# Expert layers of a macaron block on one core: gate and up in chunks of 256, 512 and 512 tokens in place of four of 320

## The reference, cut to what matters

```python
x = x + 0.5 * _L0_ffn_ref(_layernorm(x), router_w, wg, wu, wd)
x = x + _L0_attn_ref(_layernorm(x), Wq, bq, Wk, bk, Wv, bv, Wo, bo)
x = x + 0.5 * _L0_ffn_ref(_layernorm(x), router_w, wg, wu, wd)
...
def _L0_ffn_ref(x, router_w, wg, wu, wd):   # E = 8 experts, top 2, capacity 1.25 * N / E
    ...
    disp = jnp.zeros((E, capacity + 1, D), x.dtype).at[se, pos].set(xf[st])
    disp = disp[:, :capacity]
    g = jnp.einsum('ecd,edf->ecf', disp, wg)
    u = jnp.einsum('ecd,edf->ecf', disp, wu)
    eo = jnp.einsum('ecf,efd->ecd', jax.nn.silu(g) * u, wd)
    ...
    out = jnp.zeros_like(xf).at[st].add(contrib)
```

## Time and profile before

| | us |
|---|---|
| median of 3 runs | 1755.51 (1755.17 to 1757.69) |
| the profiled execution's span | 1752.8 |
| PE busy | 1586.2 |
| DVE busy | 1129.1 |
| ACT busy | 885.1 |
| POOL busy | 755.7 |

### The profile page before, as it was taken

One profiled execution on the slowest core, in us unless ns is written; L12 is line 12 of the kernel. 1 busy time (PEld: TensorE's weight loads), 2 busy tenths in 40 slices (PEclk: granted clock), 3 DMA queues, 4 the chain that ended last, 5 costly groups with the idle time before them and its releaser, 6 DMA issues.

```text
span 1752.8 us, 40278 instructions
## 1 busy us (share of the span) xinstructions
PE 1586.2 (90%) x14505; PEld 1252.3 (71%) x14505; DVE 1129.1 (64%) x2523; ACT 885.1 (50%) x1624; POOL 755.7 (43%) x611
## 2 busy tenths in 40 slices
PE   5649999999999999976899764999999999999997
PEld 4536878787877878764788653687878787777876
DVE  7898484858576574626788788746374645556461
ACT  5645454544444454527676564445454544544452
POOL 7403525344443426036666650452534444342503
PEclk9999999999999999997999755999999999999999
DMA  8754616263443525038777460452615243443502
GB/s 266 255 156 125 137 42 133 54 137 57 110 75 92 91 76 92 4 44 192 163 158 160 128 224 5 125 106 62 136 51 120 67 111 67 96 76 87 85 7 31
DMA packets 276544, 184.12 MB, mean 105 GB/s; under 512 B 175339, under 2 KB 263157, under 8 KB 276469
## 3 DMA queue, kind: packets, MB, share of 16 engines
q1 hardware_dynamic: 245748, 140.50, 29.6%
q0 software_dynamic: 30720, 42.62, 16.0%
HBM read 91.04 MB, written 55.06 MB: 83 GB/s over the span
## 4 chain that ended last, share of the span: by engine, by line
PE 78%; DVE 10%; ACT 3%; issue 3%; POOL 3%; DMA 3%; SPq 1%; DVEq 0%; POOLq 0%; ACTq 0%
PE bank L1637 48%; PE bank L1649 24%; ACT xt L763 2%; PE bank L1615 1%; PE bank L1583 1%; DVE bank L338 1%; DMA xs<-x_d 1%; DVE xn L1046 1%; PE bank L1690 1%; DVE xn L1135 1%; POOL rows L530 1%; PE bank L1525 1%; POOL w_d L540 1%; POOL unit_buf L535 1%; PE bank L1722 1%
## 5 line engine op out<-in xcount | busy, mean ns | idle before, releaser
L1637 PE MATMUL bank<-xT,rows 128*128 128x320 f16 x3072 | 500.5, 299 | 1.0 <-DVE w_u L1025 1.0
L1637 PE MATMUL bank<-xT,w_u 128*128 128x320 f16 x3072 | 500.8, 299 | 0.0
L1262 DVE SCALAR_TENSOR_TENSOR unit_buf<-bank,sc_cur,unit_buf 128x320 f32<-128x320 f32 x512 | 281.9, 551 | 327.3 <-PE bank L1637 318.6
L812 ACT ACTIVATE unit_buf<-bank,sc_cur 128x320 f32<-128x320 f32 x512 | 269.5, 526 | 375.4 <-PE bank L1637 373.2
L1649 PE MATMUL bank<-w_d,xs 128*128 128x256 f16 x3840 | 421.8, 273 | 0.0
L1649 PEld LDWEIGHTS bank<-w_d,xs 128*128 128x128 f16 x3840 | 375.7, 98 | 44.3
L1637 PEld LDWEIGHTS bank<-xT,w_u 128*128 128x128 f16 x3072 | 300.6, 98 | 116.7
L1637 PEld LDWEIGHTS bank<-xT,rows 128*128 128x128 f16 x3072 | 291.6, 98 | 109.6 <-issue 2.0
L460 POOL DMA_INDIRECT gat<-rows_d,id_next x160 | 183.3, 1146 | 311.1 <-issue 253.9
L1268 DVE TENSOR_TENSOR xs<-unit_buf,xs 128x320 f16<-128x320 f32 x512 | 246.9, 482 | 2.2
L818 ACT ACTIVATE xs<-unit_buf 128x320 f16<-128x320 f32 x512 | 235.6, 460 | 10.4 <-DVE unit_buf L1262 10.4
(11 more groups left out here) (238 smaller groups left out, 1618.7 us busy)
## 6 DMA issues: line engine op xcount, KB each, us to landing
rows_d<-rows SPq DMA_DIRECT2D x32, 512.0 KB, 3.7
raw_gu<-in_L_ffn_wg SPq DMA_DIRECT2D x16, 1024.0 KB, 6.7
raw_gu<-in_L_ffn_wu SPq DMA_DIRECT2D x16, 1024.0 KB
raw_d<-in_L_ffn_wd SPq DMA_DIRECT2D x16, 1024.0 KB, 5.2
x_d<-xs SPq DMA_DIRECT2D x1, 8192.0 KB, 32.8
out_x<-xs SPq DMA_DIRECT2D x16, 512.0 KB, 3.5
xs<-in_L_attn_x SPq DMA_DIRECT2D x7, 1024.0 KB, 7.4
xs<-x_d SPq DMA_DIRECT2D x6, 1024.0 KB, 6.4
```

The lines of the kernel that those rows point to most:

```text
L812: act.activation(act_s[:, u % 2, :], bank[u % 2][:, 0:CW], ACT.Silu, scale=sc_cur[:, 3:4]).then_inc(S.s_ready, 1)
L1262: dve.scalar_tensor_tensor(h32[:, u % HB, :], bank[2 + u % 2][:, 0:CW], sc_cur[:, 4:5], act_s[:, u % 2, :], mult, mult).then_inc(S.h32_rea ...
L1637: mm = pe.matmul(bank[2 * m + u % 2][:, 0:CW], wgu[m][:, w, k, f * P:(f + 1) * P], xT[:, a * KD + k, c * CW:(c + 1) * CW], start=(j == 0 a ...
```

## The change

The three chunks are of two, four and four row blocks: 256, 512 and 512 tokens, so an expert has 24 units. PE issues 96 matmuls of 256 columns and 192 of 512 for gate and up, where it issued 384 of 320. `act_s` moves from `unit_buf` to `xn`, and `h32` takes all of `unit_buf`. The first expert begins on two row blocks turned by PE, and each weight's split is awaited by itself, just before its first matmul. The down weight's split moves to units 8 to 12, and the list pieces, maxima, list read and gathers get new unit numbers.

```diff
-    CH = 4
-    CW = C // CH
+    CHUNKS = ((0, 2), (2, 6), (6, 10))
+    CH = len(CHUNKS)
+    SPAN = [slice(a * P, z * P) for a, z in CHUNKS]
+    CW = max(z - a for a, z in CHUNKS) * P
...
-    BY_PE = 3
-    PARTS = ((0, 1), (2,), (3, 4), (5, 6, 7), (8, 9))
+    BY_PE = 2
+    PARTS = ((0, 1), (2, 3), (4, 5), (6, 7), (8, 9))
+    CHUNK_OF = [c for c, (a, z) in enumerate(CHUNKS) for _ in range(a, z)]
...
-        AMAX_JOIN = 25
-        AMAX_AT = {u: (k // 4, k % 4) for k, u in enumerate((7, 10, 13, *range(16, 25)))}
-        PIECE_AT = {5 + i + i // 2: i for i in range(LP)}
+        AMAX_AT = {11: (0,), 16: (1, 2), 17: (3,), 18: (4, 5), 19: (6, 7), 20: (8, 9), 21: (10, 11)}
+        AMAX_JOIN = 22
+        PIECE_AT = {u: i for i, u in enumerate((2, 4, 6, 8, 10, 13, 14, 15))}
...
-        READ_AT = 20
+        READ_AT = 18
+        DOWN_HI_AT = (8, 11)
+        DOWN_LO_AT = (9, 12)
...
-                            pool.wait_ge(S.u_ready, units + READ_AT + 2 + s)
+                            pool.wait_ge(S.u_ready, units + READ_AT + 1 + s // 2)
...
-                        if units is not None and (s == 0 or READ_TILL[s] > READ_TILL[s - 1]):
-                            sp.wait_ge(S.u_ready, units + FT * (READ_TILL[s] + 1))
+                        if units is not None and s == CHUNKS[c][0]:
+                            sp.wait_ge(S.u_ready, units + FT * (c + 1))
...
-                act.activation(act_s[:, u % 2, :], bank[u % 2][:, 0:CW], ACT.Silu,
+                w = wide(u)
+                act.activation(act_s[:, u % 2, 0:w], bank[u % 2][:, 0:w], ACT.Silu,
...
-                    if u in (0, FT // 2):
-                        pe.wait_ge(S.gu_lo, 4 * e + (2 if u == 0 else 4))
-
                     for m, (free, done) in enumerate(((S.s_ready, S.g_ready), (S.h32_ready, S.u_ready))):
                         pe.wait_ge(free, UNITS * e + u + 1)
+                        if u in (0, FT // 2):
+                            pe.wait_ge(S.gu_lo, 4 * e + 2 * (u > 0) + m + 1)
                         for j, (a, w) in enumerate(HALVES):
                             for k in range(KD):
-                                mm = pe.matmul(bank[2 * m + u % 2][:, 0:CW], wgu[m][:, w, k, f * P:(f + 1) * P],
-                                               xT[:, a * KD + k, c * CW:(c + 1) * CW],
+                                mm = pe.matmul(bank[2 * m + u % 2][:, 0:wide(u)], wgu[m][:, w, k, f * P:(f + 1) * P],
+                                               xT[:, a * KD + k, SPAN[c]],
```

More of the change, by code:

```diff
@@ L324, in col, with wide @@
             return ap[:, i:i + n] if isinstance(i, int) else ap[:, bass.ds(i, n)]
+        def wide(u):
+            a, z = CHUNKS[u // FT]
+            return (z - a) * P
         def wait_for(eng, sm, n):
@@ L626, in turn_rows @@
                     for s in blocks:
-                        c = NEEDED_BY[s]
-                        if units is not None and (s == 0 or READ_TILL[s] > READ_TILL[s - 1]):
-                            sp.wait_ge(S.u_ready, units + FT * (READ_TILL[s] + 1))
+                        c = CHUNK_OF[s]
+                        if units is not None and s == CHUNKS[c][0]:
+                            sp.wait_ge(S.u_ready, units + FT * (c + 1))
                             settle(sp)
-                        if units is not None and s and NEEDED_BY[s - 1] < c:
-                            sp.wait_ge(turned[c - 1], 16 * NEEDED_BY.count(c - 1) * (n + S.first + 1))
-                            settle(sp)
+                            if c:
+                                sp.wait_ge(turned[c - 1], 16 * CHUNK_OF.count(c - 1) * (n + S.first + 1))
+                                settle(sp)
                         sp.dma_start_transpose(xT[:, :, s * P:(s + 1) * P], gat[:, s, 0:2 * D]).then_inc(turned[c], 16)
@@ L1261, in unit @@
                 dve.wait_ge(S.h_ready, UNITS * e + u + 1)
[L1262 to L1263 removed]
+                w = wide(u)
+                dve.scalar_tensor_tensor(h32[:, u % HB, 0:w], bank[2 + u % 2][:, 0:w], sc_cur[:, 4:5],
+                                         act_s[:, u % 2, 0:w], mult, mult).then_inc(S.h32_ready, 1)
             def unit_lo(S, e, u):
@@ L1297, in expert @@
                         continue
-                    if u in AMAX_AT and not S.scaled:
-                        m, i = AMAX_AT[u]
-                        ch.mark(weight_amax(S, m, n, i))
+                    for k in () if S.scaled else AMAX_AT.get(u, ()):
+                        ch.mark(weight_amax(S, k // 4, n, k % 4))
                     if u in PIECE_AT:
@@ L1659, in ffn @@
                 spin(bank[7], wgu[0][:, 0, 0, 0:512], 12)
-                for j in range(2):
-                    pe.wait_ge(gathered[j], 16 * len(PARTS[j]) * (S.first + 1))
-                    for s in PARTS[j]:
-                        for c in range(2 * KD):
-                            i = pe.transpose(bank16[s][:, c * P:(c + 1) * P], gat[:, s, c * P:(c + 1) * P], ident16[:, :])
-                        i.then_inc(S.counted, 1)
-                    spin(bank[7], wgu[0][:, 0, 0, 0:512], 2)
+                pe.wait_ge(gathered[0], 16 * len(PARTS[0]) * (S.first + 1))
+                for s in PARTS[0]:
+                    for c in range(2 * KD):
+                        i = pe.transpose(bank16[s][:, c * P:(c + 1) * P], gat[:, s, c * P:(c + 1) * P], ident16[:, :])
+                    i.then_inc(S.counted, 1)
+                spin(bank[7], wgu[0][:, 0, 0, 0:512], 2)
                 with pe.Fori(0, E - 1) as e:
```

38 lines of the change are left out of this document (18 added, 20 removed).

## The result

The changed kernel takes 1792.0 us (median of 4 runs, 1788.5 to 1793.7), the kernel before 1755.96 beside it: a ratio of 1.0199, 95% interval 1.0187 to 1.021. That is 36 us slower. The forecast was 4 us slower, 1759.6 us, and its range ended at 1766. The sign was right and the size wrong by a factor of nine; nearly all of the loss lies where the prediction said "no gap during down parts". The profiled execution of the changed kernel spans 1786.7 us, against 1752.8 before: 33.9 us to find.

A forecast was written before the change was run, and what follows sets the result against it. TensorE was taken to bound the kernel, at 90% of the span. One pass: 1.4 + 6 x 0.15 - 0.25 = 2.05, two passes 4.1, so 1755.51 becomes 1759.6 us; range 1754 to 1766.

The forecast's parts named there:

- no gap during down parts: Down parts of the experts: PE would show no gap there, nor at chunk starts.
- Step 1: Gate and up of each expert: fewer, wider matmuls take 51.91 us in place of 52.16, a gain of 4.0 in all.
- Step 2: Gate and up units: VectorE and ScalarE keep up with 512-wide units, and 256-wide ones are close but covered; price 0.
- Step 3: First expert: PE starts earlier, at about 136.9, gaining 0.65 us, with some 0.17 given back at up of unit 2.
- step 4: First expert of each pass: PE waits 2.1 us for POOL's hot_v at the first list piece; the expert is 1.4 longer.
- Step 5: Six middle experts per pass: PE waits 0.40 us for hot_v at the first list piece, net +0.15 each.
- rival A: POOL is in time in the middle experts and only the first experts wait: -0.7, 1754.8 us; chance 19%.
- Step 6: Moved transposes, gathers, scatters and weight scales around the down part cost nothing: price 0, margin 1.7 us.
- The scales are ready about 9.8 into it: Pass 1: weight scales come about 9.8 us into the down part; PE needs block 3's eviction only if after about 11.5.
- rival C: Another wait starts: scales later than 11.5 in pass 1, hot_v blocked, or VectorE behind; about 1766 us; chance 14%.
- The scatters catch up: Down part: gathers end about 4 us into it; scatters have 2.62 us each for 1.9 of work.

The follow-up runs named there:

- g4: Changed kernel with list pieces moved to units 6 to 10 and 13 to 15, and the weight maxima's two transfers one row pair earlier in SP's queue: 1749.9 us, ratio 0.9984.
- e4: Changed kernel with list pieces at units 5 to 12 and the list read at unit 15, so gathers come earlier: 1749.3 us, ratio 0.9983.
- g3: Changed kernel with list pieces at units 5 to 12 and the list read at unit 15, run on another chip: 1749.8 us, ratio 0.9981.
- h3: Changed kernel with list pieces at units 5 to 12 and the list read at unit 15, run in the last job: 1749.8 us, ratio 0.9984.
- e2: Changed kernel with list pieces moved to units 6 to 10 and 13 to 15, gathers left where they are: 1776.4 us, ratio 1.0138.
- f1: Changed kernel unaltered, run again on a third chip: 1780.4 us, ratio 1.0146.
- g1: Changed kernel unaltered, run again on a fourth chip: 1780.7 us, ratio 1.0157.
- h1: Changed kernel with only the weight maxima's two transfers moved one row pair earlier in SP's queue: 1757.5 us, ratio 1.0028.
- e1: Changed kernel with list pieces at units 2, 4, 5 to 10 and the list read at unit 13, so gathers come earlier: 1756.0 us, ratio 1.0021.

## Why the prediction was wrong

**Step 1, right.** Gate and up of the last expert: 51.91 forecast, 51.92 measured. In g4 the middle experts take 53.52, 0.25 less than 53.77. The kernels without waits (e4, g3, g4, h3) show this gain in their times: ratios of 0.9981 to 0.9984, some 3 us of the forecast 4.0.

**Step 2, right.** No product, split or PSUM bank holds gate and up: 1.5 us idle for all 4608 matmuls of L1647. Chunk 1 was turned in time.

**Step 3, right within the run's own shift.** VectorE's first split begins at 135.71, 0.57 later than in the earlier trace rows, and PE at 137.57. From 136.9 + 0.57 that is 0.1 off. Timeline of PE in the changed kernel, and with it the first list piece of step 4:

```profile
137.57 0.83 PE L1647 MATMUL bank<-xT,rows 128*128 128x256 f16 x6 [0.79 <-issue]
...
144.82 1.01 POOL L468 DMA_INDIRECT gat<-rows_d,id_next  x1 [0.30 <-issue]
145.85 0.47 POOL L458 TENSOR_TENSOR hot_v<-hot_b,val 128x160 bf16<-128x160 bf16 x1
...
146.47 0.35 PE L1626 MATMUL bank<-hot_v,hot_a 128*128 128x20 bf16 x8 [1.98 <-issue]
```

**Step 4, right, the number in part by luck.** Forecast: PE waits 2.1 us, to 146.0; measured 1.98, to 146.47, which is 145.9 without the shift. Three errors cancel: the last gather starts 0.3 later than forecast (144.82 against 143.96 + 0.57), hot_v takes 0.47 and not 0.83, and PE starts 0.15 behind its end, not 0.05. The second pass has it too. The first expert's gate and up last 55.90 us (53.77 before); in e2, where the wait is gone, 53.75.

**Step 5, right mechanism, wrong size.** In the twelve middle experts POOL's hot_v waits for the landing of the last scatter, as said. But the forecast wait of 0.40 is mostly missing: gate and up of nine of the twelve last 53.52 to 53.66, which is rival A (53.52), and of three 54.0 to 54.3. The average of 53.72 lies midway between A and the forecast 53.92. The failed term is hot_v's duration. Timeline of a middle expert, pieces 0 and 1, then the durations in ns (minimum, median, maximum):

```profile
312.39 0.45 POOL L458 TENSOR_TENSOR hot_v<-hot_b,val 128x160 bf16<-128x160 bf16 x1 [2.82 <-DMA x_d<-xs,id_cur]
...
314.26 0.68 DVE L1241 TENSOR_TENSOR hot_a<-pos_a,slot_a 128x1024 bf16<-128x1024 bf16 x1
314.42 0.84 POOL L458 TENSOR_TENSOR hot_v<-hot_b,val 128x160 bf16<-128x160 bf16 x1 [1.58 <-DVE hot_b L1239]
```

```profile
L458 POOL TENSOR_TENSOR hot_v<-hot_b,val x112: 450/836/839, 145.8 to 1651.6; 128x160 bf16<-128x160 bf16 x112
```

Before, all 112 took 828 to 838 ns, and I took the steadiness for a sign that nothing lengthens hot_v. It was the reverse. In all 112 of the kernel before hot_v begins 0.16 to 0.18 us behind a hot_a on VectorE and ends 0.31 to 0.32 behind its end. In the changed kernel that holds for 98; the fourteen first pieces, which POOL reaches late, meet no hot_a and take 0.45 to 0.51. The rule that I weighed and set aside (the Trainium skill, SBUF — State Buffer, "SBUF: two separate sides": VectorE instructions with two SBUF inputs and GpSimd instructions lock each other out) agrees with both rows, 0.45 alone and 0.84 beside hot_a, and would have given a wait near 0, not 0.40.

**Step 6, wrong, and it holds the result.** Two statements failed.
- "The scales are ready about 9.8 into it", margin 1.7. The mechanism (rival C, given 14% together with two others) was right, and so was the threshold of 11.5 within 0.3: in the seven parts of f1 and the seven of g1 PE waits as long as the scales come behind +11.2 to +11.3. The term was mis-sized: the scales come at +13.1 to +16.7 in f1, and in the part shown above at +14.7, 4.9 us later than forecast, where PE waits 3.31. The prediction gives no working for 9.8 but "the gathers' new times", so what it counted is not known; what the runs show is that the maxima's first transfer stands on SP behind the landing of the first chunk's transposes and behind two more transposes. In g4, where it follows the join of the maxima at once, the scales come at +8.9 to +11.1. Seven such parts are 22 to 28 us. Rival C's "1 us each for every us beyond" also left out the clock, below.
- "No gap during down parts." In the jobs with stops there is at least one in every down part but each pass's last, of no semaphore, which no row of before announced: L1649 had 0.0 idle. Why they are there stays open.

"The scatters catch up" was right: in g4 the gathers run into the down part and nothing comes of it.

**The sum.** Forecast: +4.1. In the jobs without stops the profiled spans of f1 and g1 lie 32.7 and 26.0 above the median spans of the kernel before beside them (1751.4 and 1750.8). The down parts hold 28.2 and 21.7 of that, and 4.5 and 4.3 remain for what was forecast. h1, which has the forecast's terms and nearly no wait for the scales, is 4.1 us slower by the medians (1757.47 against 1753.35; 3 to 7 us by its ratio's interval). So what the prediction counted came out, as far as these runs can tell. In the first result: +33.9 by the spans, of which 33.1 in the down parts. That the sign was right owes little to the forecast's terms: they are 4 of the 36 us. One bound of the sum is wrong as it stands: with waits of 0 in the middle experts the lower end is 2 x (1.1 - 7 x 0.25) = -1.3, not +1.7; the stated range of 1754 to 1766 covers it.

## What to carry to other kernels

When gathers or loads move, list everything that stands behind them in the queue that waits for their landing, and follow the last of it to the engine that needs it; here two small transfers behind transposes, and behind a wait for earlier ones to land, cost 23 of the 28 us that the changed kernel loses where it has no stops (g1). A chunk boundary that moves can carry such a wait to a new place in the queue. An instruction whose duration never varies may always be waiting for the same neighbour: ask what runs beside it before carrying the duration to another place. Where a loss has no semaphore, run the unchanged kernel again beside every variant, and on another chip, before explaining it: e1 to e4 alone would have made a false case against the list pieces.
